# A graph network of four layers on one core: which chunks of the last layer are multiplied, and which engine makes the one-hot tiles and copies the first quarter out of PSUM

## The chip, the cores and the metric

The kernel runs on one core of a Trainium2 chip. The metric is device time in microseconds (us): the median of the runs of the whole kernel. A core has TensorE (PE; PEld is its weight load), VectorE (DVE), ScalarE (ACT), GpSimd (POOL) and SyncE (SP). Each works through its own instructions in order, and they wait for each other by semaphores.

## The reference

A graph of 3125 nodes with 64 features and 53125 edges (`src`, `dst`, sorted by `dst`) goes through four layers. Each begins with `h = relu(layernorm(x))` and ends by adding its result to `x`. Layers 0 to 2 are a weighted mean over neighbours, an attention layer and a layer with two batch norms. The last one, layer 3, is the one that the change touches:

```python
def _L3_gnn_ref(x, edge_index):
    msgs = x[edge_index[1]]
    return jax.ops.segment_sum(msgs, edge_index[0], num_segments=x.shape[0])

edge_index = jnp.stack([src, dst])
h = jnp.maximum(_layernorm(x, axis=-1), 0.0)
x = x + _L3_gnn_ref(h, edge_index)
```

The edges are listed in both directions and with loops, so this is the sum over each node's neighbours and itself, and the kernel computes it as the sum, over the edges of each `dst`, of the row of `src`.

## The kernel before

**Chunks.** The edges, sorted by their target node, are cut into two halves, which lie on partitions 0 to 63 and 64 to 127 (64 features each). Each half is cut into 52 chunks of 512 edges (`NCH`, `CH`). A chunk of layer 3 needs the table row `h[src]` of each of its 2 x 512 edges as a tile of 128 x 512 (channels by edges). VectorE then runs a segmented scan along the edges (`l3_scan`: state times `keep` plus the new value, carried from chunk to chunk in `scan_ring`, two buffers), TensorE transposes the result back (`l3_out`, PSUM banks 6 and 7), ScalarE copies it out (`evacuate`) and SyncE stores it (`store_scan`). When all are stored, GpSimd fetches the last row of each node (`last_rows`), VectorE adds it to `x`, and SyncE stores the output.

**Two ways to the rows.** A chunk is *fetched* or *multiplied*; `MULTIPLIED[3]` lists the multiplied ones (21 of 52 before: those with c % 5 in 1 and 3), `FETCHED[3]` the other 31.

- Fetched: GpSimd issues eight indirect DMAs of 128 rows each (`gather_chunk`), four chunks ahead at most, and TensorE transposes the rows into PSUM bank 4 or 5 (`l3_in`: four transposes of 128x128), from which the scan reads them.
- Multiplied: the table, split into an upper and a lower part (`parts[3]`), lies in SBUF. Its 25 blocks of 128 nodes are grouped by four: seven groups (`NU`), group u with blocks 4u to 4u+3. For each group a one-hot tile of 128 x 1024 (two halves of 512 edges) says which row of the group, modulo 128, an edge wants. TensorE multiplies (`multiply`): for one half of the edges 26 products of 128x512, four for each of groups 0 to 5 and two for group 6, in the order of u, into two banks (0 and 1 for the first half, 2 and 3 for the second). The two banks hold four candidates per edge, the quarters. The first quarter is copied to `rows[m % 2]`, and `pick` overwrites it with `copy_predicated` where one of the other three is meant (three instructions of 64x512 for each half).

**One-hot tiles.** VectorE makes a tile with one `tensor_scalar` (is_equal, `make_onehots`, L1657 with a small accumulator read behind it). ScalarE makes one with two instructions, Abs of the distance (L1184) and Relu of one minus it (L1195), in `distances_and_onehots`. `ACT_U[3]` and `DVE_U[3]` say who makes which: before, ScalarE tiles 1 and 4, VectorE tiles 0, 2, 3, 5, 6. There are two sets of seven tiles, so the tiles of chunk m+1 are made while chunk m is multiplied.

**The order on each engine**, for the m-th multiplied chunk c (all orders are written out by hand; nothing overtakes within an engine):

- TensorE: `multiply` of the first half; `l3_out` of the chunks from the previous multiplied one up to c-1; `multiply` of the second half; `l3_in` of the fetched chunks up to the next multiplied one. Before each tile's products it waits for that tile, and before each half for the previous chunk's copy and picks of that half.
- VectorE: `pick` of the first half; all its tiles of chunk m+1 but the last; `pick` of the second half; scan of c; the last of its tiles of m+1 (`DVE_U[3][-1:]`); scans of the chunks up to the next multiplied one. `pick` waits for the quarters' masks and for the first quarter's copy.
- ScalarE: `first_quarter` of the first half (L1203, PSUM to `rows`); `evacuate` (L1026) of the chunks from the previous multiplied one up to c-1; `distances_and_onehots` of chunk m+1; `first_quarter` of the second half.
- SyncE: loads of row indices (`load_rows`, three multiplied chunks ahead in layer 3, behind a wait for the tiles of m+1) and of the quarters' masks (`load_quarters`), and a store for each chunk.

Layer 2 has the same scheme with 20 multiplied chunks and its own lists. Lines: L600 gather, L634 last rows, L897 products, L989 `l3_out`, L999 `l3_in`, L1666 `copy_predicated`, L1769 the scan of layer 3. In layer 0, L738 and L746 are transposes of TensorE.

Of the kernel before, what the change touches and what calls it, by code (L numbers as in the profile page):

```python
# [37 lines left out]
NCH = HALF // CH  # L38
# [15 lines left out]
NFIRST = 4  # L54

NU = -(-NB // 4)
MULTIPLIED = {2: [c for c in range(NCH) if c % 13 in (1, 3, 6, 8, 11)], 3: [c for c in range(NCH) if c % 5 in (1, 3)]}
FETCHED = {layer: [c for c in range(NCH) if c not in some] for layer, some in MULTIPLIED.items()}
ACT_U = {2: (2, 5), 3: (1, 4)}
DVE_U = {layer: tuple(u for u in range(NU) if u not in some) for layer, some in ACT_U.items()}  # L60
NW = NBP * D
NV = NB * D
# [8 lines left out]
def build(nc, T, out):  # L71
    ctx = ExitStack()
    with ctx:
# [5 lines left out]
        def S(name, slot=None):  # L79

            key = name if slot is None else f"{name} [{slot}]"
            if key not in sems:
                sems[key] = ctx.enter_context(nc.semaphore(key.replace(" ", "_").strip("]").replace("[", "")))
            return sems[key]
# [21 lines left out]
        def n_chunks(before, n, each=1):  # L106
            return past(n + before * NIT, each)
# [9 lines left out]
        def tile(layer, m, u):  # L117

            sets = len(onehot[layer]) // NU
            return onehot[layer][m % sets * NU + u]  # L120
# [6 lines left out]
        def after(layer, m):  # L127

            some = MULTIPLIED[layer] + [NCH]
            return range(some[m] + 1, some[m + 1])  # L130
# [7 lines left out]
        def n_scanned(layer, n):  # L138
            return n_chunks(layer, n)
# [115 lines left out]
        P = ctx.enter_context(nc.psum_tensor("psum", [128, 8, 512], F32))  # L255
# [47 lines left out]
        quarter = [spared(3 * CH // 4).bitcast(U8).rearrange("p (q e) -> p q e", q=3) for _ in range(2)]  # L303
        rows = [spared(CH) for _ in range(2)]
# [62 lines left out]
        halves = (slice(0, 64), slice(64, 128))  # L367
# [4 lines left out]
        def _(sp):  # L372
# [126 lines left out]
            def load_rows(layer, m):  # L499

                if m >= 2:
                    sp.wait_ge(S(f"L{layer} DVE onehots made"), (m - 1) * len(DVE_U[layer]))
                    if ACT_U[layer]:
                        sp.wait_ge(S(f"L{layer} distances made"), (m - 1) * len(ACT_U[layer]))
                c = MULTIPLIED[layer][m]
                for hf in range(2):
                    sp.dma_start(rowb[m % 2][:, hf * CH:(hf + 1) * CH],
                                 src_row[hf, c * CH:(c + 1) * CH].partition_broadcast(128)) \
                        .then_inc(S(f"L{layer} rows loaded", m % 2), 16)

            def load_quarters(layer, m):
                if m >= 2:
                    sp.wait_ge(S(f"L{layer} quarters picked", 1), m - 1)
                for hf in range(2):
                    sp.dma_start(quarter[m % 2][halves[hf], :, :],
                                 quarter_dram[hf, MULTIPLIED[layer][m]].partition_broadcast(64)) \
                        .then_inc(S(f"L{layer} quarters loaded", m % 2), 16)
# [14 lines left out]
            for c in range(NCH):  # L532
                m = MULTIPLIED[2].index(c) if c in MULTIPLIED[2] else None
                if m is not None and m + 2 < len(MULTIPLIED[2]):
                    load_rows(2, m + 2)
# [128 lines left out]
        def _(pe):  # L664
# [219 lines left out]
            def multiply(layer, m, hf, bank):  # L884

                if m:
                    pe.wait_ge(S(f"L{layer} first quarter copied", hf), m)
                    pe.wait_ge(S(f"L{layer} quarters picked", hf), m)
                for u in range(NU):
                    if u in ACT_U[layer]:  # L890
                        pe.wait_ge(S(f"L{layer} ACT onehots made"), m * len(ACT_U[layer]) + ACT_U[layer].index(u) + 1)
                    else:
                        pe.wait_ge(S(f"L{layer} DVE onehots made"), m * len(DVE_U[layer]) + DVE_U[layer].index(u) + 1)
                    for t in range(2):
                        b = 4 * u + 2 * t
                        for n in range(len(parts[layer]) if b < NB else 0):
                            last = nc.tensor.matmul(P[:, bank + t, :],  # L897
                                                    parts[layer][n][:, b:b + 2, :].rearrange("p b d -> p (b d)"),
                                                    tile(layer, m, u)[:, hf * CH:(hf + 1) * CH],
                                                    start=(u == 0 and n == 0), stop=(b + 4 >= NB and n == len(parts[layer]) - 1))  # L900
                    if hf == 1:
                        last.then_inc(S(f"L{layer} onehots used"), 1)
                if hf == 0:
                    last.then_inc(S(f"L{layer} first half multiplied"), 1)
# [29 lines left out]
            for m, c in enumerate(MULTIPLIED[2]):  # L934
                multiply(2, m, 0, 4)
                if m == 0:
                    l2_chunk(0)
                l2_chunk(c)
                multiply(2, m, 1, 6)
                for other in after(2, m):  # L940
                    l2_chunk(other)
# [75 lines left out]
        def _(act):  # L1017
# [157 lines left out]
            def distances_and_onehots(layer, m):  # L1175

                made = m * len(ACT_U[layer])
                temps = distance[layer]
# [16 lines left out]
                    nc.scalar.activation(tile(layer, m, u), temps[(made + n) % len(temps)], ACT.Relu, scale=-1.0, bias=1.0) \  # L1195
                        .then_inc(S(f"L{layer} ACT onehots made"), 1)

            def first_quarter(layer, m, hf, bank):
                if hf == 0:
                    act.wait_ge(S(f"L{layer} first half multiplied"), m + 1)  # L1200
                else:
                    act.wait_ge(S(f"L{layer} onehots used"), (m + 1) * NU)
                nc.scalar.activation(rows[m % 2][halves[hf], :], P[0:64, bank, :], ACT.Copy) \  # L1203
                    .then_inc(S(f"L{layer} first quarter copied", hf), 1)

            def copy_eaT(c):
                i, k = c // 2, c % 2
# [4 lines left out]
            def l2_chunk(c):  # L1212
                i, k = c // 2, c % 2
                if c + 1 < NCH:
                    copy_eaT(c + 1)
                if c in FETCHED[2]:
                    act.wait_ge(S("hidden summed", k), past(n_same(FETCHED[2], c)))
                else:
                    act.wait_ge(S("ea product made", k), past(i + 1))
                nc.scalar.activation(arena[:, at(i, k)], P[:, 2 + k, :], ACT.Identity, bias=cols[:, LB1:LB1 + 1]) \  # L1220
                    .then_inc(S("hidden made", k), 1)
# [3 lines left out]
            for m, c in enumerate(MULTIPLIED[2]):  # L1225
                if m >= 2:
                    act.wait_ge(S("rows added"), m - 1)
                first_quarter(2, m, 0, 4)
                if m == 0:
                    l2_chunk(0)  # L1230
                l2_chunk(c)
                if m + 1 < len(MULTIPLIED[2]):
                    distances_and_onehots(2, m + 1)
                first_quarter(2, m, 1, 6)
                for other in after(2, m):
                    l2_chunk(other)

# [33 lines left out]
            for part in PARTS:  # L1271
                c = slice(PAIRS[part].start * 128, PAIRS[part].stop * 128)
# [4 lines left out]
            act.wait_ge(*stage("z activated b"))  # L1277
            distances_and_onehots(3, 0)
            for m, c in enumerate(MULTIPLIED[3]):
                if m >= 2:  # L1280
                    before = MULTIPLIED[3][m - 2]
                    act.wait_ge(S("scanned", before % 2), n_scanned(3, before // 2 + 1))
                first_quarter(3, m, 0, 0)
                for before in range(MULTIPLIED[3][m - 1] if m else 0, c):
                    evacuate(3, before // 2, before % 2, 6 + before % 2)
                if m + 1 < len(MULTIPLIED[3]):
                    distances_and_onehots(3, m + 1)
                first_quarter(3, m, 1, 2)
            for c in range(MULTIPLIED[3][-1], NCH):
                evacuate(3, c // 2, c % 2, 6 + c % 2)  # L1290

# [2 lines left out]
        def _(dve):  # L1294
            v = nc.vector
            steps = [0]

            def step(ins):

                steps[0] += 1  # L1300
                ins.then_inc(S("dve step"), 1)
                dve.wait_ge(S("dve step"), steps[0])
# [358 lines left out]
            def pick(layer, m, hf, bank):  # L1661

                dve.wait_ge(S(f"L{layer} quarters loaded", m % 2), 32 * (m // 2 + 1))
                dve.wait_ge(S(f"L{layer} first quarter copied", hf), m + 1)
                for q in range(1, 4):
                    picked = v.copy_predicated(rows[m % 2][halves[hf], :], quarter[m % 2][halves[hf], q - 1, :],  # L1666
                                               P[halves[q % 2], bank + q // 2, :])
                    if q < 3:
                        step(picked)
                picked.then_inc(S(f"L{layer} quarters picked", hf), 1)  # L1670
# [140 lines left out]
```

## Time and profile before

| | us |
|---|---|
| median of the 3 runs | 2159.79 (2159.34 to 2163.71) |
| profiled execution | 2162.31 |
| its span, first to last instruction | 2160.6 |
| busy: PE / DVE / ACT / POOL | 1405.2 / 1539.8 / 779.1 / 1403.9 |
| TensorE's granted clock, share of full speed | 0.751 |
| layer 3's multiplications (L897), first to last start | 1781.7 to 2110.5 |

The page's chain of work that ended last is made of TensorE 19%, GpSimd 11%, VectorE 8% of the span, with L897 (14%) and L600 (8%) as the largest lines. A row of a timeline gives start, length, engine, line, operation, output and input, the number of instructions that are merged, and in brackets how long the engine had been idle and what ended that. A row of groups gives busy time, the mean length of one in ns, and the idle time before them. PE's busy time is modelled, and its instructions overlap: where a distance counts, it is taken from start to start.

### The profile page before, as it was taken

How to read it: one execution, taken by the hardware profiler on the slowest of the kernel's cores; microseconds unless marked ns; L12 is line 12 of the kernel's file. 1: busy time of each engine (PE TensorE's matmuls, PEld its weight loads, DVE VectorE, ACT ScalarE, POOL GpSimd, SP SyncE). 2: the span in 40 equal slices, each digit the busy share in tenths (PEclk: the TensorE clock that was granted, in tenths of full speed). 3: DMA queues.
4: the chain of work that ended last, by engine and by line, in shares of the span. 5: the costliest groups of instructions: out<-in, count | busy, mean ns of one | idle time of the engine just before them, and what ended most of it. 6: DMA issues, size and time to landing. Idle time of an engine off the chain costs nothing. (4 is left out here: it accounts for less than half of the span.)

```text
span 2160.6 us, 22803 instructions
## 1 busy us (share of the span) xinstructions
PE 1405.2 (65%) x6447; PEld 1099.0 (51%) x6447; DVE 1539.8 (71%) x2405; ACT 779.1 (36%) x1056; POOL 1403.9 (65%) x1468
## 2 busy tenths in 40 slices
PE   2777777778444444444443179999977428999991
PEld 1555555555433433334333057777754216777770
DVE  6877777777547777777776667777768456998882
ACT  1333333333123434334333045445546313444430
POOL 5777777777627777777774467777710317777754
PEclk9866666676666665566665589999985558999995
DMA  5322232222224544444443243444434303333331
GB/s 131 85 81 75 80 85 79 71 85 81 59 79 138 159 146 154 151 151 156 147 153 130 54 95 91 95 91 100 97 88 160 121 20 77 92 104 101 99 85 40
DMA packets 214866, 220.83 MB, mean 102 GB/s; under 512 B 107694, under 2 KB 167555, under 8 KB 214531
## 3 DMA queue, kind: packets, MB, share of 16 engines
q1 hardware_dynamic: 163971, 143.64, 21.9%
q0 software_dynamic: 47072, 62.55, 13.4%
q10 hardware_dynamic: 3744, 13.63, 1.6%
q8 instruction: 43, 0.70, 0.1%
q14 instruction: 36, 0.29, 0.0%
HBM read 118.24 MB, written 101.46 MB: 102 GB/s over the span
## 5 line engine op out<-in xcount | busy, mean ns | idle before, releaser
L600 POOL DMA_INDIRECT gathered<-table,idx x1336 | 1287.7, 964 | 536.0 <-issue 409.5
L897 PE MATMUL psum<-rounded 128*128 128x512 f32 x1092 | 265.2, 400 | 23.7 <-DVE rounded L1657 23.7
L1666 DVE COPY_PREDICATED spare<-spare,psum 64x512 f32<-64x512 uint8 x246 | 181.4, 737 | 111.7 <-ACT spare L1203 105.1
L859 PE MATMUL psum<-ident,arena 128*128 128x128 f32 x208 | 57.9, 434 | 293.8 <-ACT arena L1145 293.8
L897 PEld LDWEIGHTS psum<-rounded 128*128 128x128 f32 x1092 | 206.3, 192 | 66.4 <-issue 24.1
L634 POOL DMA_INDIRECT arena<-scan,rowidx x100 | 102.5, 1025 | 191.2 <-DMA scan<-ea 125.0
L859 PEld LDWEIGHTS psum<-ident,arena 128*128 128x128 f32 x208 | 37.2, 217 | 307.9 <-issue 171.5
L1203 ACT ACTIVATE spare<-psum 64x512 f32<-64x512 f32 x82 | 48.3, 589 | 320.1 <-PE psum L897 319.6
L1048 ACT ACTIVATE arena<-psum 128x1024 f32<-128x1024 f32 x52 | 53.2, 1023 | 241.6 <-PE psum L724 150.0
L1156 ACT ACTIVATE arena<-arena 128x1024 f32<-128x1024 f32 x52 | 54.9, 1056 | 226.2 <-DVE arena L1584 226.2
L1657 DVE TENSOR_SCALAR_CACHE_REDUCE rounded<-spare,rowcol 128x1024 fp32r<-128x1024 uint16 x105 | 128.3, 1264 | 0.0
L897 PE MATMUL psum<-rounded_keep 128*128 128x512 f32 x480 | 127.9, 415 | 0.0
L738 PE MATMUL psum<-ident,arena 128*128 128x128 f32 x416 | 100.6, 388 | 39.6 <-DVE arena L1435 19.6
L1444 DVE TENSOR_TENSOR arena<-gathered,wgt 128x512 f32<-128x512 f32 x52 | 36.3, 699 | 113.4 <-DMA gathered<-table,idx 113.4
L738 PEld LDWEIGHTS psum<-ident,arena 128*128 128x128 f32 x416 | 69.0, 197 | 93.6 <-issue 48.3
L746 PE MATMUL psum<-ident,arena 128*128 128x128 f32 x208 | 51.8, 397 | 89.0 <-DVE scan_ring L1452 60.2
L732 PEld LDWEIGHTS psum<-W,arena 128*128 128x128 f32 x416 | 105.1, 329 | 5.1
L897 PEld LDWEIGHTS psum<-rounded_keep 128*128 128x128 f32 x480 | 89.8, 190 | 27.0 <-issue 9.6
L851 PE MATMUL psum<-ident,arena 128*128 128x128 f32 x416 | 97.9, 416 | 5.3 <-DVE arena L1598 5.3
L732 PE MATMUL psum<-W,arena 128*128 128x128 f32 x416 | 101.2, 401 | 0.0
L1571 DVE TENSOR_TENSOR arena<-psum,arena 128x512 f32<-128x512 f32 x52 | 35.9, 690 | 89.8 <-PE psum L859 89.8
L1145 ACT ACTIVATE arena<-gathered 128x1024 f32<-128x1024 f32 x52 | 55.0, 1057 | 110.8 <-DMA gathered<-table,idx 110.8
(257 smaller groups left out, 3195.2 us busy)
## 6 DMA issues: line engine op xcount, KB each, us to landing
scan<-arena SPq DMA_DIRECT2D x52, 768.0 KB, 3.6
scan<-ostage SPq DMA_DIRECT2D x130, 256.0 KB, 2.2
gathered<-table,idx POOLq DMA_INDIRECT x1336, 2.6
d_mlp<-arena ACTq DMA_DIRECT2D x26, 512.0 KB, 2.7
arena<-d_mlp SPq DMA_DIRECT2D x52, 256.0 KB, 2.7
ea<-in_edge_attr SPq DMA_DIRECT2D x104, 128.0 KB
spare<-src_row SPq DMA_DIRECT2D x82, 128.0 KB, 3.2
spare<-src_quarter SPq DMA_DIRECT2D x82, 96.0 KB, 3.1
```

What stands on the lines that cost most here:

```text
L600: pool.indirect_dma_start(out=out[:, j, hf, :], out_offset=None, in_=tab[layer], in_offset=bass.IndirectOffsetOnAxis(ap=idx[:, j, hf * NCH ...
L634: pool.indirect_dma_start(out=agg[:, b * width:(b + 1) * width], out_offset=None, in_=segs[layer], in_offset=bass.IndirectOffsetOnAxis(ap= ...
L732: last = nc.tensor.matmul(P[:, 2 + k, j * 128:(j + 1) * 128], y1[k][:, j::J], W[:, WD2, :], start=False, stop=True, skip_group_check=True)
L738: last = nc.tensor.transpose(P[:, 4, j::J], mlp[layer][:, k * CH + j * 128:k * CH + (j + 1) * 128], ident[:, :])
L851: last = nc.tensor.transpose(P[:, 3 + n, j * 128:(j + 1) * 128], run[:, j::J], ident[:, :])
L859: last = nc.tensor.transpose(P[:, 0, j::J], wsplit[k][:, j * 128:(j + 1) * 128], ident[:, :])
L897: last = nc.tensor.matmul(P[:, bank + t, :], parts[layer][n][:, b:b + 2, :].rearrange("p b d -> p (b d)"), tile(layer, m, u)[:, hf * CH:(h ...
L1048: nc.scalar.activation(square[layer], PF[:, layer * 2 * CH:(layer + 1) * 2 * CH], ACT.Square) \
L1145: nc.scalar.activation(wsplit[k].rearrange("p (n r d) -> p r n d", n=2, d=D), Gring[k][:, :].rearrange("p (r n d) -> p r n d", n=2, d=D), ...
L1156: nc.scalar.activation(soft[k], soft[k], ACT.Exp).then_inc(S("expd made", k), 1)
L1657: v.tensor_scalar(tile(layer, m, u), rowb[m % 2], rowcol[:, 0, u:u + 1], None, ALU.is_equal, ALU.add, accum_out=small[:, 6, u:u + 1]) \
L1666: picked = v.copy_predicated(rows[m % 2][halves[hf], :], quarter[m % 2][halves[hf], q - 1, :], P[halves[q % 2], bank + q // 2, :])
```

## The change

`MULTIPLIED[3]` has the chunks with c % 9 in 1, 3, 5, 7: 23 chunks, the last is 50, and 29 are fetched. ScalarE makes tiles 1, 2, 4, 5, 6 of layer 3, VectorE 0 and 3. The first quarter of layer 3 is copied by VectorE at the start of `pick`, which waits for TensorE itself; TensorE no longer waits for that copy, and ScalarE's loop loses its two copies and a wait for the scan. Layer 2 keeps its scheme; TensorE's wait for the copy goes there too.

```diff
-MULTIPLIED = {2: [c for c in range(NCH) if c % 13 in (1, 3, 6, 8, 11)], 3: [c for c in range(NCH) if c % 5 in (1, 3)]}
+MULTIPLIED = {2: [c for c in range(NCH) if c % 13 in (1, 3, 6, 8, 11)], 3: [c for c in range(NCH) if c % 9 in (1, 3, 5, 7)]}
 FETCHED = {layer: [c for c in range(NCH) if c not in some] for layer, some in MULTIPLIED.items()}
-ACT_U = {2: (2, 5), 3: (1, 4)}
+ACT_U = {2: (2, 5), 3: (1, 2, 4, 5, 6)}
...
             def multiply(layer, m, hf, bank):
                 if m:
-                    pe.wait_ge(S(f"L{layer} first quarter copied", hf), m)
                     pe.wait_ge(S(f"L{layer} quarters picked", hf), m)
...
             for m, c in enumerate(MULTIPLIED[3]):
-                if m >= 2:
-                    before = MULTIPLIED[3][m - 2]
-                    act.wait_ge(S("scanned", before % 2), n_scanned(3, before // 2 + 1))
-                first_quarter(3, m, 0, 0)
                 for before in range(MULTIPLIED[3][m - 1] if m else 0, c):
                     evacuate(3, before // 2, before % 2, 6 + before % 2)
                 if m + 1 < len(MULTIPLIED[3]):
                     distances_and_onehots(3, m + 1)
-                first_quarter(3, m, 1, 2)
...
             def pick(layer, m, hf, bank):
                 dve.wait_ge(S(f"L{layer} quarters loaded", m % 2), 32 * (m // 2 + 1))
-                dve.wait_ge(S(f"L{layer} first quarter copied", hf), m + 1)
+                if layer == 2:
+                    dve.wait_ge(S("L2 first quarter copied", hf), m + 1)
+                else:
+                    if hf == 0:
+                        dve.wait_ge(S("L3 first half multiplied"), m + 1)
+                    else:
+                        dve.wait_ge(S("L3 onehots used"), (m + 1) * NU)
+                    step(v.tensor_copy(rows[m % 2][halves[hf], :], P[0:64, bank, :]))
```

## Rows read from the trace of the kernel before

**Rows 1.** Window in layer 3: PE, PEld, DVE, ACT, POOL busy, clock, DMA.

```profile
1900.00:1940.00 40.00, 37.59 (x182) 31.04 (x181) 36.12 (x49) 18.58 (x24) 30.55 (x32) 1.00 0.41 107
```

**Rows 2.** Groups by line and shape, from 1770 to 2110 us.

```profile
L897 PE MATMUL psum<-rounded 128*128 128x512 f32 x1089 | 264.6, 400 | 23.7 <-DVE rounded L1657 23.7
L600 POOL DMA_INDIRECT gathered<-table,idx x248 | 241.1, 972 | 117.9 <-issue 73.4 <-DMA table<-arena 42.7 <-PE psum L999 1.8
...
L1184 ACT ACTIVATE arena<-spare,rowcol 128x1024 f32<-128x1024 uint16 x40 | 43.6, 1141 | 0.0
L1195 ACT ACTIVATE rounded<-arena 128x1024 fp32r<-128x1024 f32 x40 | 39.9, 1047 | 0.0
...
L1647 DVE CAST rounded<-arena 128x1664 fp32r<-128x1664 f32 x1 | 1.0, 1028 | 0.0
```

**Rows 3.** Line of the gathers over layer 3, then its waits.

```profile
L600 POOL DMA_INDIRECT gathered<-table,idx x248: 940/944/1854, 1777.8 to 2093.2; - x124
...
PE psum L999 <- DMA gathered<-table,idx: 16.1, 9, 6.1
```

**Rows 4.** Timeline of one turn with two chunks, GpSimd left out.

```profile
1982.39 6.19 PE L897 MATMUL psum<-rounded 128*128 128x512 f32 x26
...
1988.41 0.60 PE L999 MATMUL psum<-ident,gathered 128*128 128x128 f32 x4
1988.61 0.59 ACT L1203 ACTIVATE spare<-psum 64x512 f32<-64x512 f32 x1 [0.67 <-PE psum L897]
1988.77 6.19 PE L897 MATMUL psum<-rounded 128*128 128x512 f32 x26
1989.30 2.29 DVE L1666 COPY_PREDICATED spare<-spare,psum 64x512 f32<-64x512 uint8 x3 [0.38 <-ACT spare L1203]
1991.62 1.28 DVE L1769 TENSOR_TENSOR_SCAN scan_ring<-keep,scan_ring,spare 128x512 f32<-128x512 uint8 x1
1992.82 1.25 DVE L1657 TENSOR_SCALAR_CACHE_REDUCE rounded<-spare,rowcol 128x1024 fp32r<-128x1024 uint16 x1
...
1994.80 1.40 PE L989 MATMUL psum<-ident,scan_ring 128*128 128x128 f32 x8
1995.95 6.18 PE L897 MATMUL psum<-rounded 128*128 128x512 f32 x26
1996.73 2.18 ACT L1184 ACTIVATE arena<-spare,rowcol 128x1024 f32<-128x1024 uint16 x2
```

**Rows 5.** Timeline ahead of it: the way out of three chunks.

```profile
1979.78 1.11 PE L989 MATMUL psum<-ident,scan_ring 128*128 128x128 f32 x8
1980.55 1.28 DVE L1769 TENSOR_TENSOR_SCAN scan_ring<-keep,scan_ring,psum 128x512 f32<-128x512 uint8 x1 [1.91 <-PE psum L989]
...
1981.88 0.74 PE L989 MATMUL psum<-ident,scan_ring 128*128 128x128 f32 x4 [0.99 <-DVE scan_ring L1769]
```

**Rows 6.** Group of VectorE's cast out of PSUM, in the kernel's first part.

```profile
L1358 DVE CAST idx<-psum 128x416 int32<-128x416 f32 x1 | 0.6, 592 | 0.4 <-PE psum L684 0.4
```

**Rows 7.** Timeline of PE at the loop's start.

```profile
1790.27 0.66 PE L999 MATMUL psum<-ident,gathered 128*128 128x128 f32 x4 [0.55 <-DMA gathered<-table,idx]
1792.30 1.11 PE L989 MATMUL psum<-ident,scan_ring 128*128 128x128 f32 x4 [1.37 <-DVE scan_ring L1769]
1793.06 7.50 PE L897 MATMUL psum<-rounded 128*128 128x512 f32 x26
```

**Rows 8.** Timeline of PE after its longest wait in the loop.

```profile
1820.67 1.12 PE L999 MATMUL psum<-ident,gathered 128*128 128x128 f32 x4 [6.11 <-DMA gathered<-table,idx]
1821.44 8.58 PE L897 MATMUL psum<-rounded 128*128 128x512 f32 x26
```

**Rows 9.** Timeline of PE in layer 0: two of its waits.

```profile
144.67 1.09 PE L746 MATMUL psum<-ident,arena 128*128 128x128 f32 x4 [2.48 <-DVE scan_ring L1452]
...
244.64 0.63 PE L746 MATMUL psum<-ident,arena 128*128 128x128 f32 x4 [2.36 <-DVE scan_ring L1452]
```

**Rows 10.** Timeline of PE: the last second half.

```profile
2104.70 6.18 PE L897 MATMUL psum<-rounded 128*128 128x512 f32 x26
```

More of the change, by code:

```diff
@@ L1196, in distances_and_onehots, with first_quarter @@
                         .then_inc(S(f"L{layer} ACT onehots made"), 1)
-            def first_quarter(layer, m, hf, bank):
+            def first_quarter(m, hf, bank):
                 if hf == 0:
-                    act.wait_ge(S(f"L{layer} first half multiplied"), m + 1)
+                    act.wait_ge(S("L2 first half multiplied"), m + 1)
                 else:
-                    act.wait_ge(S(f"L{layer} onehots used"), (m + 1) * NU)
+                    act.wait_ge(S("L2 onehots used"), (m + 1) * NU)
                 nc.scalar.activation(rows[m % 2][halves[hf], :], P[0:64, bank, :], ACT.Copy) \
-                    .then_inc(S(f"L{layer} first quarter copied", hf), 1)
+                    .then_inc(S("L2 first quarter copied", hf), 1)
             def copy_eaT(c):
@@ L1227, in _ @@
                     act.wait_ge(S("rows added"), m - 1)
-                first_quarter(2, m, 0, 4)
+                first_quarter(m, 0, 4)
                 if m == 0:
@@ L1233, in _ @@
                     distances_and_onehots(2, m + 1)
-                first_quarter(2, m, 1, 6)
+                first_quarter(m, 1, 6)
                 for other in after(2, m):
```

## The prediction, made before the changed kernel ran

> **What bounds the kernel now.** I began with the windows of the last layer's loop, because the change touches nothing else. There TensorE is busy 37.59 of 40 us at the full clock (2.4 GHz), VectorE 36.12, ScalarE 18.58 and GpSimd 30.55 [rows 1]. Three engines are nearly full, so what matters is which wait ends last, and for that I read the groups and the waits of the same stretch. GpSimd's 248 gathers start between 1777.8 and 2093.2 us, one per 1.27 us; what lies between them is almost all "issue", that is, nothing held them [rows 2, 3]. TensorE waits only 16.1 us for them in nine waits [rows 3]. So gathers set the pace and TensorE has some 5% of room: over ten chunks (six fetched, four multiplied) the gathers take 48 x 1.27 = 61 us.
>
> Then I followed one turn of the loop in the timeline [rows 4]. TensorE multiplies the second half of a multiplied chunk (start 1982.39), transposes the fetched chunk (1988.41), multiplies the first half of the next multiplied chunk (1988.77), and transposes two scanned chunks back (1994.80 to 1995.95). VectorE, in its own order, picks the quarters after the second half (1989.30), scans (1991.62) and then makes the one-hot tile it has kept for last (1992.82, done 1994.07). That tile is number 6, needed after 24 of the 26 products: 1988.77 + 24 x 0.232 = 1994.34 (0.232 us is 6.03 / 26, from 1988.77 to 1994.80). It comes 0.27 us early. This is the place to watch.
>
> **GpSimd.** Two chunks fewer are fetched: 16 gathers x 1.27 = 20 us less. It is a gain only if nothing else then sets the pace.
>
> **TensorE's own work.** Two more chunks are multiplied: 104 products x 0.232 = 24.1 us more, and two times four transposes of 0.09 (0.36 us per four [rows 4]) less: +23.4 us. A turn with two chunks has 6.02 + 0.36 + 6.03 + 1.15 = 13.56 us of it. A turn with three chunks has one more transpose in, and its way out takes 2.61 us (1979.78 to 1982.39), since the third scan must wait for a transpose [rows 5]: 15.38 us. In the changed kernel the 22 turns between 23 multiplied chunks are 17 of two and 5 of three: 17 x 13.56 + 5 x 15.38 = 307 us, where the same stretch is 2104.70 - 1793.06 = 311.6 us now [rows 7, 10]. The extra products alone would cost nothing; the gathers' slack pays for them.
>
> **ScalarE.** 23 x 5 = 115 pairs of Abs and Relu instead of 42, at (43.6 + 39.9) / 40 = 2.09 us [rows 2]: 240 us instead of 88, less 42 copies of 0.59. Its tiles begin 1.93 us after the transposes out (1994.80 to 1996.73 [rows 4]) and five pairs take 10.45, with some 0.2 for waits on each other, so the last is ready 12.6 us after them; TensorE asks for tile 6 at 1.15 + 6.02 + 0.36 + 5.57 = 13.1 us even with no stall. Hidden, with 0.5 us to spare; if that were gone, every microsecond would count 22 times. The Abs and Relu of ScalarE come in the order 1, 2, 4, 5, 6 and the first four have more room.
>
> **VectorE.** 23 x 2 = 46 one-hot tiles instead of 105, at 1.25 us [rows 4], saves 74 us of busy time, 46 copies add some 32. But VectorE was no bound by its sum; what counts is the order. It now keeps tile 3 for last, behind the copy, the three picks and the scan. Tile 3 is needed after 12 products, not 24.
> - A copy of 64x512 f32 out of PSUM by VectorE isn't in this trace. Nearest rows: the cast of 416 columns out of PSUM took 0.592 us [rows 6], with 96 columns more at the same slope (0.433 / 416 above a start of 0.16) 0.69; a predicated copy of the same 64x512 out of PSUM took some 0.74 (2.29 / 3, with gaps) [rows 4]; at the rate of the cast within SBUF, 1664 columns in 1.028 [rows 2], it would be 0.16 + 512 x 0.868 / 1664 = 0.43. I take 0.69, as it is the nearest in kind; 0.43 to 0.74 are the bounds. The Trainium skill (VectorE: DVE Perf Modes, Why PSUM operands drop a tier) says that f32 operands in PSUM get no faster mode; the cast agrees, and by the page the lower bound falls away.
> - From the start of a second half, results reach the next engine at 6.22 us (1982.39 to 1988.61), the copy and its wait take 0.73, and picks, scan and tile take 4.77 (1989.30 to 1994.07): tile 3 is ready at 11.72, and its products start 0.2 later with their weights, at 11.93. TensorE asks for it at 6.02 + 0.36 + 12 x 0.232 = 9.16. It waits 2.77 us, in each turn, with 14 products, the transposes and the next half behind the waiting one.
> - Turn of two: 11.93 + 14 x 0.232 + 1.15 = 16.33 us. Turn of three: 11.93 + 3.25 + 2.61 = 17.79. Sum 17 x 16.33 + 5 x 17.79 = 366.6 us.
> - The first second half still starts at 1793.06, as the tiles of chunk 1 come in time, and takes 1.32 us longer than others (7.50 against 6.18 [rows 4, 7]). So the last one starts at 1793.06 + 1.3 + 366.6 = 2161.0 instead of 2104.70: +56.3 us.
>
> **The tail.** The last multiplied chunk is 50, not 51, so chunk 51 is scanned after it: one more scan, 1.2 us (1991.62 to 1992.82), and 0.1 for VectorE's copy against ScalarE's 0.59. +1.3 us. The work behind it is as now. The waits on TensorE for the first quarter's copy go, at nothing, since the picks' own wait comes later. The load of row indices on SyncE waits for the same last tile as before, two turns ahead of its use: hidden.
>
> **The clock.** The stalls are short, but the trace shows that such gaps cost more than themselves. After gaps of 0.55 and 1.37 us the clock fell to 1.2 GHz: four transposes took 1.11 instead of 0.75 and the next half 7.50 instead of 6.18, 1.7 us together [rows 5, 7]. After 6.11 us idle it cost (1.12 - 0.60) + (8.58 - 6.18) = 2.9 [rows 4, 8]. In layer 0 there is one wait of 2.1 to 2.6 us in most turns of about 20 us: of 18 such waits between 121 and 525 us, 13 were followed by slow or partly slow transposes (0.90 to 1.09 us for four) and 5 by fast ones (0.63) [rows 9]. Each has a shorter wait of some 0.8 us ahead of it, which the stalls here lack; but these are the only waits of the stalls' size at the full clock. By that share 16 of the 22 stalls lower the clock. I take 2.0 us for each, nearer to the shorter gap: 16 x 2.0 = 32 us. Bounds: none, 0; all at 2.3 (the mean of both), 51. It adds in full, as the slow products lie on the same loop.
>
> Against the profiled run's span, 2160.6 + 56.3 + 1.3 + 32 = 2250; that run took 2162.31 us in all, 2.5 above the median of the runs, which I scale to: 2159.8 + 90 = 2250 us.
>
> **Rivals.**
> 1. The stall comes, the clock doesn't fall: 2159.8 + 57.6 = 2217 us. For it: in the last layer eight of the nine waits for gathers, (16.1 - 6.1) / 8 = 1.25 us each, lie in stretches at the full clock [rows 1, 3]. Against it: layer 0's waits of the stall's own size. The Trainium skill (TensorE: Matmul & The Clock Gate, HAM oscillation — how this bites in real kernels) tells of a kernel that is throttled anew in every turn, after waits of 3 to 5 us; ours would be shorter than those, so by the page this rival would be the likelier, and layer 0's rows speak against it. 15%.
> 2. The clock falls at nearly every stall, and stays down longer: 22 x 2.3 = 51 us give 2268. 12%.
> 3. Not slower: tile 3 comes in time. VectorE would have to have it 2.8 us earlier, as if the picks and the scan had been overtaken; it decides from a chain of under 2.7 us after the second half's results, where 5.5 are worked out. Then TensorE's turns add to 307 us, and with 1.3 at the start and 1.3 for the tail the end is at 2159.8 - 2: 2158 us, within 0.2%, with the gathers 20 us ahead and idle. Nothing in the rows breaks VectorE's order. 5%. A gain above 0.2% would need faster products too: 2%.
> 4. ScalarE comes late: its five tiles take 1 us more than worked out, and TensorE waits for tile 6 also. As tile 3's wait of 2.77 us covers it, it starts to cost only from 3 us on. Taken into the range.
>
> My forecast has 66%. A measurement of this kernel can tell 0.2% (4 us) from no change. Faster 0.02, within 0.2% 0.05, slower 0.93. The range: from rival 1 with the cheapest copy (2217 - 22 x 0.26 = 2211) to rival 2's 2268, little of which I leave out: 2211 to 2268.
>
> **What would show it.** In the changed kernel's timeline TensorE's products (the multiply line) should stand still before the 13th of each first half, 2.5 to 3 us, released by VectorE's one-hot line, 22 times, about 60 us in all; the groups should show VectorE's copy near 0.69; the windows a granted clock below 1.00 in most stretches of 10 us; gathers that wait for TensorE's transposes in; ScalarE without waits by TensorE. The prediction is wrong if the loop's multiplied chunks follow each other in 14 us, if the waits are ended by ScalarE, or if the clock stays at 1.00.

## The result, and the profile after

The changed kernel takes 2230.82 us (median of 4 runs, 2228.68 to 2236.5), the one before 2159.57 us beside it: 1.0333 times as long, 95% interval 1.0311 to 1.0355, or 71 us more. The profiled execution took 2230.53 us, its span is 2228.7 us. In the changed code L896 are the products, L1665 VectorE's copy of the first quarter, L1667 the picks, L1651 its one-hot tiles, L1770 the scan, L988 and L998 the transposes out and in, L1183 and L1194 ScalarE's Abs and Relu.

A window of the loop comes first (columns as in rows 1: PE, PEld, DVE, ACT, POOL busy, clock, DMA share, GB/s):

```profile
1860.00:1880.00 20.00, 17.52 (x76) 14.01 (x75) 12.98 (x18) 13.79 (x15) 15.12 (x17) 0.91 0.38 91
...
2000.00:2020.00 20.00, 17.50 (x83) 14.28 (x82) 13.54 (x19) 15.49 (x17) 13.06 (x14) 1.00 0.42 111
```

In [rows 1] TensorE had 37.59 of 40 us and the full clock; now it has 17.5 of 20, which is 35 of 40, and in 15 of the 20 stretches of 20 us between 1780 and 2180 the granted clock is 0.90 to 0.96. VectorE is no longer nearly full (13 of 20), GpSimd has become idle in places. No engine is full: the loop runs at the pace of a chain. The waits between 1770 and 2190 us name it (us in total, times, longest):

```profile
DVE spare L1665 <- PE psum L896: 117.7, 40, 3.9
PE psum L896 <- DVE rounded L1651: 75.0, 23, 23.7
POOL gathered L600 <- issue: 67.2, 220, 0.5
POOL gathered L600 <- PE psum L998: 65.6, 11, 8.3
```

TensorE waits for VectorE's tiles 23 times; without the first, the loop's start, which stands in [rows 2] as well, these are 22 waits and 51.3 us. None of them was there before. The gathers have turned round: they waited 1.8 us for TensorE's transposes [rows 2] and wait 65.6 us now. The timeline of two turns shows the wait and what may follow it:

```profile
1946.29 6.17 PE L896 MATMUL psum<-rounded 128*128 128x512 f32 x26
1952.30 0.60 PE L998 MATMUL psum<-ident,gathered 128*128 128x128 f32 x4
1952.56 0.68 DVE L1665 COPY spare<-psum 64x512 f32<-64x512 f32 x1 [2.69 <-PE psum L896]
1952.65 3.00 PE L896 MATMUL psum<-rounded 128*128 128x512 f32 x12
1953.28 2.30 DVE L1667 COPY_PREDICATED spare<-spare,psum 64x512 f32<-64x512 uint8 x3
1955.62 1.30 DVE L1770 TENSOR_TENSOR_SCAN scan_ring<-keep,scan_ring,spare 128x512 f32<-128x512 uint8 x1
1956.84 1.25 DVE L1651 TENSOR_SCALAR_CACHE_REDUCE rounded<-spare,rowcol 128x1024 fp32r<-128x1024 uint16 x1
1958.15 5.09 PE L896 MATMUL psum<-rounded 128*128 128x512 f32 x14 [2.51 <-DVE rounded L1651]
1963.08 1.11 PE L988 MATMUL psum<-ident,scan_ring 128*128 128x128 f32 x8
1963.94 6.19 PE L896 MATMUL psum<-rounded 128*128 128x512 f32 x26
...
1970.32 3.00 PE L896 MATMUL psum<-rounded 128*128 128x512 f32 x12
...
1975.83 3.48 PE L896 MATMUL psum<-rounded 128*128 128x512 f32 x14 [2.51 <-DVE rounded L1651]
1979.14 1.11 PE L988 MATMUL psum<-ident,scan_ring 128*128 128x128 f32 x8
1980.01 6.17 PE L896 MATMUL psum<-rounded 128*128 128x512 f32 x26
```

Where 26 products followed each other [rows 4], they are cut after the twelfth. The chain is to be read off on VectorE: copy, picks, scan, tile, and then at once the thirteenth product (1956.84 + 1.25 = 1958.09, start 1958.15). Both groups of 14 waited for 2.51 us. The first took 5.09 us, at the lowered clock (1.2 GHz), the second 3.48, at 2.4 GHz. A turn takes 1963.94 - 1946.29 = 17.65 us with such a slow group and 1980.01 - 1963.94 = 16.07 without, against 13.56 before. 12 of the 22 turns have a slow group. The wait is about 2.5 us in the turns of two chunks, 2.05 in the five of three, and 1.04 in the first turn.

From the first second half to the last it is 2171.32 - 1790.53 = 380.8 us, 69.2 more than the 311.6 of before [rows 7, 10]. The start is 2.5 us earlier in this trace and the tail 1.5 longer (57.4 against 55.9): 68.1 us, the difference of the two spans.

### The profile page after: what moved, and what is told of

The parts are those of the page before. It is cut to its first block and busy times, and to the rows that moved or that the text cites. A ratio compares the mean times of both kernels' runs of the same rounds, so it can differ in the third digit from the quotient of the medians.

```text
span 2228.7 us, 23094 instructions
## 1 busy us (share of the span) xinstructions
PE 1442.8 (65%) x6543; PEld 1125.3 (50%) x6543; DVE 1509.0 (68%) x2345; ACT 906.0 (41%) x1160; POOL 1386.0 (62%) x1452
## 5 line engine op out<-in xcount | busy, mean ns | idle before, releaser
L600 POOL DMA_INDIRECT gathered<-table,idx x1320 | 1268.9, 961 | 592.4 <-issue 402.8
L896 PE MATMUL psum<-rounded 128*128 128x512 f32 x1196 | 311.9, 417 | 75.0 <-DVE rounded L1651 75.0
L896 PEld LDWEIGHTS psum<-rounded 128*128 128x128 f32 x1196 | 234.5, 201 | 133.9 <-DVE rounded L1651 60.5
L1667 DVE COPY_PREDICATED spare<-spare,psum 64x512 f32<-64x512 uint8 x258 | 190.9, 740 | 98.8 <-ACT spare L1202 91.3
L1025 ACT ACTIVATE ostage<-psum 128x512 f32<-128x512 f32 x104 | 59.7, 596 | 172.7 <-PE psum L988 158.4
L896 PE MATMUL psum<-rounded_keep 128*128 128x512 f32 x480 | 128.2, 416 | 0.0
L1183 ACT ACTIVATE arena<-spare,rowcol 128x1024 f32<-128x1024 uint16 x115 | 127.1, 1147 | 1.5
L1194 ACT ACTIVATE rounded<-arena 128x1024 fp32r<-128x1024 f32 x115 | 115.5, 1042 | 0.0
L1665 DVE COPY spare<-psum 64x512 f32<-64x512 f32 x46 | 31.3, 680 | 117.7 <-PE psum L896 117.7
L896 PEld LDWEIGHTS psum<-rounded_keep 128*128 128x128 f32 x480 | 90.0, 191 | 27.1 <-issue 9.6
```

Of the source, the lines that this page charges most:

```text
L600: pool.indirect_dma_start(out=out[:, j, hf, :], out_offset=None, in_=tab[layer], in_offset=bass.IndirectOffsetOnAxis(ap=idx[:, j, hf * NCH ...
L896: last = nc.tensor.matmul(P[:, bank + t, :], parts[layer][n][:, b:b + 2, :].rearrange("p b d -> p (b d)"), tile(layer, m, u)[:, hf * CH:(h ...
L1025: nc.scalar.activation(ostage[k][:, :, :, :].rearrange("p h j d -> p j h d"), P[:, bank, :].rearrange("p (j h d) -> p j h d", h=2, d=D), A ...
L1183: nc.scalar.activation(temps[(made + n) % len(temps)], rowb[m % 2], ACT.Abs, bias=rowcol[:, 1, ACT_U[layer][n]:ACT_U[layer][n] + 1]).then_ ...
```

## The experiments

Each is the changed kernel with one edit, or, where it is said, the kernel before. The first four ran on one chip, where the kernel before took 2160.00 us (19 runs).

**e1. Both tiles of VectorE between the picks.**

```diff
                 if more:
-                    make_onehots(3, m + 1, DVE_U[3][:-1])
+                    make_onehots(3, m + 1, DVE_U[3])
                 pick(3, m, 1, 2)
                 l3_scan(c)
-                if more:
-                    make_onehots(3, m + 1, DVE_U[3][-1:])
```

> The changed kernel with one edit: VectorE makes both its tiles (0 and 3) between the picks of the two halves, none behind the scan. My theory (the loss is TensorE's wait for tile 3, which VectorE keeps behind copy, picks and scan, and the clock that falls after it): the 22 waits of 2.0 to 2.5 us and the 12 slow groups go, turns of 13.3 and 15.3 us, together some 303 instead of 381 us: about 2155 us. Rival (the 104 added products, 24 us, and ScalarE's 240 us of tiles are on the path): no better than 2180. Rival (VectorE's copy of 0.68 us is the cost): 46 x 0.68 = 31 us stay lost, 2190.

Measured: 2156.32 us (10 runs), ratio to before 0.9981 (0.9970 to 0.9992). The same instructions as in the changed kernel, on the same engines, and some 74 us less than the changed kernel. Its timeline, one turn:

```profile
1930.86 6.17 PE L896 MATMUL psum<-rounded 128*128 128x512 f32 x26
...
1933.17 1.26 DVE L1651 TENSOR_SCALAR_CACHE_REDUCE rounded<-spare,rowcol 128x1024 fp32r<-128x1024 uint16 x1
...
1934.36 1.27 DVE L1651 TENSOR_SCALAR_CACHE_REDUCE rounded<-spare,rowcol 128x1024 fp32r<-128x1024 uint16 x1
...
1937.13 0.68 DVE L1665 COPY spare<-psum 64x512 f32<-64x512 f32 x1 [1.50 <-PE psum L896]
1937.22 6.18 PE L896 MATMUL psum<-rounded 128*128 128x512 f32 x26
...
1943.24 1.11 PE L988 MATMUL psum<-ident,scan_ring 128*128 128x128 f32 x8
...
1944.11 6.17 PE L896 MATMUL psum<-rounded 128*128 128x512 f32 x26
```

Both tiles are done by 1935.6, while VectorE would have waited for the second half anyway; it still waits 1.50 us before the copy. The 26 products run through, and a turn takes 13.25 us. So neither the added products, nor ScalarE's load, nor the copy on VectorE is the loss: it is the place of one tile in VectorE's order. The small gain over the kernel before is what the change gives in this order with 23 chunks. TensorE is then full:

```profile
1920.00:1960.00 40.00, 39.01 (x193) 32.79 (x192) 31.67 (x42) 32.23 (x35) 30.86 (x31) 1.00 0.40 99
```

**e2. VectorE makes tiles 0 and 6, ScalarE 1 to 5.**

```diff
-ACT_U = {2: (2, 5), 3: (1, 2, 4, 5, 6)}
+ACT_U = {2: (2, 5), 3: (1, 2, 3, 4, 5)}
```

> The changed kernel with ScalarE making tiles 1 to 5 and VectorE 0 and 6; as many tiles on each engine as in the changed kernel, and VectorE still keeps its last one behind the scan, but that is tile 6, which TensorE needs after 24 products and not after 12. Theory (place of the late tile): ready 11.7 us after the second half's start, asked for at 11.95: no wait for VectorE; ScalarE's tile 5 is now asked for after 20 products, at about the time it is ready, which may cost 0.1 to 0.3 us a turn. 2157 to 2165 us. Rival (the number of tiles or the copy, not the place): as the changed kernel, 2231.

Measured: 2164.84 us (10 runs), ratio 1.0020 (1.0011 to 1.0030). The last tile may stay behind the scan if it is the one that TensorE needs last. What is left is again a wait for tile 3, which ScalarE now makes as its third:

```profile
1907.14 0.60 ACT L1025 ACTIVATE ostage<-psum 128x512 f32<-128x512 f32 x1 [2.06 <-DMA scan<-ostage]
...
1912.29 3.00 PE L896 MATMUL psum<-rounded 128*128 128x512 f32 x12
...
1915.03 2.94 ACT L1194 ACTIVATE rounded<-arena 128x1024 fp32r<-128x1024 f32 x3
...
1916.12 3.54 PE L896 MATMUL psum<-rounded 128*128 128x512 f32 x14 [0.83 <-ACT rounded L1194]
...
1926.75 6.43 PE L896 MATMUL psum<-rounded 128*128 128x512 f32 x26
```

The products stop behind the twelfth until ScalarE's third Relu is done (it starts at 1915.03 and takes 1.04). This turn waits 0.83 us; behind the other turns of three chunks it is 0.60 to 0.83. There ScalarE starts its tiles late, since its third copy out of the chunks before has waited some 2 us for a store. The other turns lose about 0.25 us (6.43 instead of 6.18), at the 13th and 14th product too. I had expected the loss at tile 5: the total lies within my range, but by another tile.

**e3. Ten products of no use in each wait** (zeros as weights, added to the running sum, so that TensorE works while it would have waited).

```diff
                 for u in range(NU):
+                    if layer == 3 and hf == 0 and m and u == 3:
+                        for n in range(10):
+                            nc.tensor.matmul(P[0:64, bank, :], parts[3][1][:, NB, :], tile(3, m, 2)[:, 0:CH],
+                                             start=False, stop=False, skip_group_check=True)
```

> The changed kernel with ten more products of TensorE in each of the 22 waits for tile 3 (64 rows of zeros as weights, so the sums stay as they are), 10 x 0.232 = 2.3 us. TensorE does useless work where it waited, and nothing else is changed. Theory: the wait itself stays paid, but the clock no longer falls: 12 x 1.55 = 19 us less, 2212 us, granted clock 1.00 in the loop. Rival (the products behind a wait are slow for another cause, such as ScalarE and VectorE writing at the same time): 2231, with some groups of 14 products still at 5.0 us.

Measured: 2212.43 us (4 runs), ratio 1.0235 (1.0218 to 1.0252): 18.4 us less than the changed kernel, though TensorE has 220 products more. Three lines of a turn (L901 are the products, L892 the added ones), and a window:

```profile
1928.09 3.00 PE L901 MATMUL psum<-rounded 128*128 128x512 f32 x12
1930.92 2.47 PE L892 MATMUL psum<-rounded 128*64 128x512 f32 x10
1933.58 3.48 PE L901 MATMUL psum<-rounded 128*128 128x512 f32 x14 [0.19 <-DVE rounded L1656]
```

```profile
1840.00:1880.00 40.00, 38.81 (x187) 30.89 (x186) 26.09 (x35) 29.22 (x31) 30.43 (x32) 1.00 0.38 95
```

The wait is still paid, with work that nobody needs, but from 1820 us on every window of the loop has the clock at 1.00 (the first, from 1780, has 0.97), and the groups of 14 take 3.4 to 3.5 us. A turn of two chunks takes 16.05 us (1921.71 to 1937.76), as the turns of the changed kernel without a slow group, so the added products cost nothing of their own. This tells the two parts of the loss apart: 18.4 us come from the clock, the rest from the wait itself.

**e4. The division of labour alone, with the 21 chunks of before.**

```diff
-3: [c for c in range(NCH) if c % 9 in (1, 3, 5, 7)]
+3: [c for c in range(NCH) if c % 5 in (1, 3)]
```

> Only the division of labour of the change, with the 21 multiplied chunks of the kernel before. Theory: the wait comes with the division, not with the chunks: 20 turns, ten of 16.1 and ten of 17.8 us, and the clock falls in about 11 of them: 339 + 17 = 356 us where the kernel before has 312: 2204 us. Rival (the two added chunks carry the loss): 2160.

Measured: 2200.63 us (4 runs), ratio 1.0179 (1.0162 to 1.0196). The wait and 41 of the 71 us come without the added chunks. The other 30 us come with them: there are 22 turns at the slow pace instead of 20, and 12 slow groups instead of six. The total is 3 us under what I expected. The clock fell less often than I had assumed, behind six of the 18 waits that were longer than 2 us; one group behind such a fall and one without (start, length, products):

```profile
2017.12 5.07 PE L896 MATMUL psum<-rounded 128*128 128x512 f32 x14 [2.48 <-DVE rounded L1651]
...
2121.80 3.50 PE L896 MATMUL psum<-rounded 128*128 128x512 f32 x14 [2.48 <-DVE rounded L1651]
```

**e5 and e10. Tile 3 ahead of the scan.** From here on seven of eight runs fell on two chips on which every kernel took some 27% longer, the kernel before too (2764 and 2732 us): in stretches of some 6 to 30 us one product of TensorE came every 1.4 to 2.8 us, at times later still, with nothing in the program to wait for. Between these stretches the loop runs as on the others. I therefore read single undisturbed turns of these runs, and take no total from them.

```diff
                 pick(3, m, 1, 2)
-                l3_scan(c)
                 if more:
                     make_onehots(3, m + 1, DVE_U[3][-1:])
+                l3_scan(c)
```

> The changed kernel with VectorE making tile 3 ahead of the chunk's scan instead of behind it. This takes one scan, 1.25 us, out of the chain behind the second half: the wait becomes about 1.2 us (0.8 in a turn of three chunks) instead of 2.5 (2.05), in 22 turns. Theory for the clock (it falls only behind the longer waits; waits of 1.4 us left it up): no group of 14 products at 5.0 us, turns of 14.8 and 16.6 us: 46 us less than the changed kernel, 2185 us. Rival (the clock falls after any wait that comes in each turn, if more seldom): 6 to 12 slow groups stay, 2194 to 2204.

> The kernel with tile 3 ahead of the scan, on an ordinary chip. Theory: waits of about 1.3 us in the turns of two chunks (0.8 in those of three), no slow group of 14 products: 2185 us. Rival (the clock falls after any wait that comes in each turn): 6 to 12 slow groups, 2194 to 2204 us.

Measured: 1.0001 (0.9975 to 1.0027) and 1.0013 (0.9976 to 1.0051) times the kernel before on those two chips. The totals say nothing of the 2185 us. An undisturbed turn of the second run:

```profile
2331.72 6.19 PE L896 MATMUL psum<-rounded 128*128 128x512 f32 x26
...
2341.05 1.28 DVE L1651 TENSOR_SCALAR_CACHE_REDUCE rounded<-spare,rowcol 128x1024 fp32r<-128x1024 uint16 x1
...
2342.40 3.48 PE L896 MATMUL psum<-rounded 128*128 128x512 f32 x14 [1.31 <-DVE rounded L1651]
2343.63 1.28 DVE L1770 TENSOR_TENSOR_SCAN scan_ring<-keep,scan_ring,psum 128x512 f32<-128x512 uint8 x1
2345.72 1.11 PE L988 MATMUL psum<-ident,scan_ring 128*128 128x128 f32 x8
...
2346.58 6.17 PE L896 MATMUL psum<-rounded 128*128 128x512 f32 x26
```

The wait is 1.31 instead of 2.51 us, the turn 14.86 instead of 16.07: one scan out of the chain, 1.2 us out of the turn. Behind the 24 waits of 0.86 to 1.32 us in both runs every group of 14 took 3.5 us; slow ones stood only behind the disturbances, after 4 us and more. That the wait gets shorter by one scan is shown by these turns; the total on an ordinary chip is not.

**e6 and e9. 22 multiplied chunks, both tiles between the picks.** The edit of e1 and:

```diff
-3: [c for c in range(NCH) if c % 9 in (1, 3, 5, 7)]
+3: [c for c in range(NCH) if c % 7 in (1, 3, 5)]
```

> Both tiles of VectorE between the picks, and 22 multiplied chunks (c % 7 in 1, 3, 5), 30 fetched. With 23 TensorE is full (39 of 40 us) and the gathers have slack; with 21 the gathers were the bound. Worked out from the turns of the kernel with 23: 14 turns of 13.25 and 7 of 15.43 us, 293.5 us where 23 chunks took 306.1, so 12 us less from TensorE: 2145 us; the gathers, 240 x 1.27 = 305 us from 1777.8, end at 2083 and allow the same within 2 us. Theory (two bounds that cross between 21 and 23): 2143 to 2148, faster than both kernels. Rival (something else holds the loop, such as ScalarE's tiles): 2155, as with 23.

> The kernel with both tiles between the picks and 22 multiplied chunks once more, since on the chip of the run before every kernel, that of before too, took some 600 us longer with long waits that no kernel explains. As before: TensorE's turns allow 2145 us, the gathers the same within 2 us: 2143 to 2148 us. Rival (something else than TensorE and the gathers holds the loop): 2155, as with 23 chunks.

Measured: e6, on a disturbed chip, 0.9950 (0.9924 to 0.9975) of before; e9, on an ordinary one, 2150.85 us (6 runs) against 2160.09, ratio 0.9960 (0.9947 to 0.9974). It is faster than both kernels, by 9 us against the one before, and misses my 2143 to 2148 by 3 us. The difference is in the start of its loop, where the gathers are not yet ahead:

```profile
1797.96 0.66 PE L998 MATMUL psum<-ident,gathered 128*128 128x128 f32 x4 [1.24 <-DMA gathered<-table,idx]
...
1828.47 1.11 PE L998 MATMUL psum<-ident,gathered 128*128 128x128 f32 x4 [3.34 <-DMA gathered<-table,idx]
1829.23 7.33 PE L896 MATMUL psum<-rounded 128*128 128x512 f32 x26
```

Two waits, 4.6 us, and a clock that fell behind the second (7.33 instead of 6.18). From the first second half to the last it is 300.4 us (1790.56 to 2090.95) where I had 293.5. In this order 22 chunks are 5.5 us better than the 23 of e1. 21 chunks weren't run in it, so that the bounds cross between 21 and 23 isn't shown in full.

**e7 and e12. VectorE's copy, with the old tiles (VectorE five, ScalarE 1 and 4).**

```diff
-ACT_U = {2: (2, 5), 3: (1, 2, 4, 5, 6)}
+ACT_U = {2: (2, 5), 3: (1, 4)}
```

> The changed kernel with the old division of the tiles: VectorE makes 0, 2, 3, 5, 6 and the copy of the first quarter, ScalarE 1 and 4. A turn of two chunks then has on VectorE 5 x 1.2 + 2 x (0.7 + 2.3) + 2 x 1.25 = 14.5 us against 13.25 of TensorE. If the last tile's place is what counts (6, needed after 24 products) the only loss is VectorE's own load: 17 x 14.5 + 5 x 16.2 = 328 us where the good order takes 306: 2178 us. Rival (the copy on VectorE costs nothing, as other waits cover it): 2157. Rival (it costs as in the changed kernel): 2230.

> VectorE makes the copies and still the old five tiles, 23 chunks, on an ordinary chip. Theory: the last tile's place (6) is harmless and only VectorE's load of some 14.5 us in a turn counts: 2178 us. Rival (the copy costs nothing): 2157. Rival (the loss of the changed kernel is the copy's): 2230.

Both on disturbed chips: 0.9936 (0.9909 to 0.9963) and 0.9940 (0.9904 to 0.9976) of before. An undisturbed turn of e12:

```profile
2460.29 6.18 PE L896 MATMUL psum<-rounded 128*128 128x512 f32 x26
...
2466.67 5.72 PE L896 MATMUL psum<-rounded 128*128 128x512 f32 x24
...
2472.98 0.74 PE L896 MATMUL psum<-rounded 128*128 128x512 f32 x2 [0.59 <-DVE rounded L1651]
...
2474.79 6.17 PE L896 MATMUL psum<-rounded 128*128 128x512 f32 x26
```

14.50 us a turn, as VectorE's work adds up, and the wait has moved to the last two products. So with the copy on VectorE and the old tiles a turn costs 0.9 us more than the 13.56 of before, and not 2.5. That the totals lie under the kernel before on these chips is not explained by such turns, and the 2178 us that I expected on an ordinary chip weren't measured.

**e8 and e11. The kernel before with the 23 chunks alone.**

```diff
-3: [c for c in range(NCH) if c % 5 in (1, 3)]
+3: [c for c in range(NCH) if c % 9 in (1, 3, 5, 7)]
```

> The kernel before with the 23 chunks of the change and nothing else of it. Theory (GpSimd's 20 us and TensorE's 23 us trade for each other): TensorE sets the pace with turns of 13.5 and 15.4 us, 307 us where it had 312, and the tail is one scan longer: 2157 us, no change. VectorE has 13.1 us of work and some waits for ScalarE's copies in a turn, which may push it to 2165. Rival (the added products lie on the path in full): 2183.

> The kernel before with the 23 chunks alone, on an ordinary chip. Theory (gathers and products trade for each other): 2157 us, up to 2165 if VectorE's order pushes it. Rival (the added products lie on the path in full): 2183.

Both on disturbed chips: 0.9919 (0.9891 to 0.9947) and 0.9949 (0.9919 to 0.9980) of before. Undisturbed, from second half to second half, a turn takes 13.55 us:

```profile
2553.26 6.17 PE L897 MATMUL psum<-rounded 128*128 128x512 f32 x26
...
2566.81 6.17 PE L897 MATMUL psum<-rounded 128*128 128x512 f32 x26
```

This is the 13.56 of [rows 4] with no wait in it: in such turns the chunk list costs nothing beyond its products. The list is no cause of the loss by itself; in the changed order, where each turn is slow, it adds 30 us to it (e4). Whether it gains or loses 0.2% on an ordinary chip stays open.

## Why the prediction was right, point by point

2230.82 us lies within 2211 to 2268 and 19 us under the 2250. The mechanism is the one forecast; of the terms that were off all but the tail's 0.2 us were too high, so the number didn't come out by errors that cancel.

- **The wait for tile 3.** Right in place and size. Predicted 2.77 us behind the twelfth product, 22 times. From start to start it is 1958.15 - (1952.65 + 12 x 0.232) = 2.72 us in the turns of two chunks. In the five of three it is shorter, since TensorE also asks later: this changes the wait, not the length of the turn. e1 takes it away by the order alone, e2 most of it by the tile's number alone.
- **The copy.** 0.69 us taken, 0.680 measured. The cast out of PSUM [rows 6] was the right neighbour. The rate within SBUF would have been wrong by 0.25 us. The Trainium skill (VectorE: DVE Perf Modes, Why PSUM operands drop a tier) says that f32 operands in PSUM get no faster mode, and the 0.680 us agree.
- **The turns.** 17.79 us for three chunks, 1930.23 - 1912.44 = 17.79 measured. For two, 16.33 against 16.07: I had taken over 1.15 us for the transposes out, of which 0.28 was a wait for the second scan [rows 4]. Behind the longer turn that scan is done, and they take 0.87 (1963.08 to 1963.94). Over 17 turns the 0.26 us are 4.4 us too much.
- **The start and the tail.** The 1.3 us of a slow first half didn't come (6.17 us at 1790.53). The same wait of 1.37 or 1.38 us stands there in seven traces (before, changed, e1 to e4, e9); the clock fell behind it in two, before and e1 (7.50 and 7.43 us). So the row that I took it from doesn't repeat in each trace, and what decides isn't shown. The tail grew by 1.5 for 1.3 predicted.
- **The clock.** This is the term that was mis-sized. I put 16 falls at 2.0 us, 32 us; the trace has 12 (in 21 waits over 2 us; the first was 1.04) at (5.09 - 3.48) = 1.6, 19 us, and e3 measures 18.4 by taking it away. The price was too high because I leaned towards the fall behind 6.11 us [rows 8], from which the clock came back later. The share was too high too. Layer 0's waits, which I counted, come with a second wait just ahead of them, as I had noted, and the stalls here stand alone between dense products; that this is the reason isn't shown. The length alone doesn't decide: of two waits of 2.51 us in the timeline above one was followed by slow products and one wasn't, and in e4 it was 6 of 18. What decides is open.
- **The rivals.** Rival 1, no fall at all, gave 2217: e3 is nearly that kernel, with 2212. The Trainium skill's tale of a kernel throttled in every turn (TensorE: Matmul & The Clock Gate, HAM oscillation — how this bites in real kernels) has longer waits than ours (3 to 5 us); here 2.04 to 2.51 us were enough in 12 of 21 turns. Rival 3, in which nothing is lost, didn't come; e1, with another order, shows what it would have taken: 2156 us where I wrote 2158. Rival 4 didn't appear in the changed kernel. Its like came in e2, at ScalarE's third tile and not at its last.
- **The sum.** Predicted 90 us: 56.3 + 1.3 + 32. Measured 71 by the medians and 68.1 by the spans of the two profiled executions. Of the 21.5 us between 89.6 and 68.1, 12.8 are the clock (32 against 19.2), 4.4 the transposes out, 1.3 the slow first half, and 2.5 the loop's earlier start in this one trace, which I hadn't forecast; the tail takes 0.2 back. Under 1 us is left.

## What to carry to other kernels

When work is moved between engines, the sum of busy time says little: here VectorE got 31 us less work (1539.8 to 1509.0) and the kernel took 71 us more. What decides is which instruction now stands last in an engine's order and how soon the next engine wants it; a tile kept behind a wait must be the one that is wanted last, or it must go where the engine waits anyway. A stall that comes back in each turn also makes every added turn dearer (30 us for two chunks here). A stall of TensorE should be priced with the clock that may follow it, and filling such a stall with harmless products is a cheap way to measure that part.

## What the hardware showed that I had not expected

- The clock does not fall behind every wait of the same length: of waits of 2.04 to 2.51 us between dense products 12 of 21 were followed by slow products in the changed kernel and 6 of 18 in e4; of 24 waits of 0.86 to 1.32 us none were (e5 and e10). Short waits aren't safe everywhere: at the start of the loop, where a second half follows 1.37 or 1.38 us, it was slow in two of seven traces.
- Two chips ran every kernel some 27% slower (2732 and 2764 us for the kernel before, against 2160), with stretches in which single products of TensorE came 1.4 to 2.8 us apart and nothing in the program to release them. A row of e11:

```profile
2313.42 0.58 PE L897 MATMUL psum<-rounded 128*128 128x512 f32 x1 [2.22 <-issue]
```

What holds TensorE there isn't shown by any run. But the places are not random. In all six disturbed runs with 23 chunks (e5, e7, e8, e10, e11, e12), on both chips, the 1st, 5th, 9th, 13th and 17th turn of layer 3 are the long ones: in e11 49.5, 22.8, 22.6, 22.5 and 22.9 us. This points at places in the program, not at moments in time.
